# Both ends of a slot-ordered attention and FFN kernel written out as one list per engine

## The reference, cut to what matters

```
x = x + xattn(layernorm(x), ctx, mask)      # softmax over 120 keys, masked scores set to 1e-9
x = x + ffn(layernorm(x))
def bitlinear(x, w, b):                     # activations to 8 bit per row, weights to -1, 0, 1
    xq = act_quant(rmsnorm(x));  wq = weight_quant(w)
    return einsum('bsd,fd->bsf', xq, wq) + b
ffn(x) = bitlinear(gelu(bitlinear(x, w1, b1)), w2, b2)
```

## Time and profile before

| | |
|---|---|
| runs | 709.9, 712.62, 714.48 us; median 712.62 |
| the profiled execution | 713.07 us; span 711.3 us |
| mean granted TensorE clock | 0.988 |
| busy, share of the span | TensorE 92%, VectorE 83%, ScalarE 74%, GpSimd 72% |

### The profile page before, as it was taken

One profiled execution on the slowest core, in us unless ns is written; L12 is line 12 of the kernel. 1 busy time (PEld: TensorE's weight loads), 2 busy tenths in 40 slices (PEclk: granted clock), 3 DMA queues, 4 the chain that ended last, 5 costly groups with the idle time before them and its releaser, 6 DMA issues.

```text
span 711.3 us, 13969 instructions
## 1 busy us (share of the span) xinstructions
PE 653.6 (92%) x4894; PEld 428.6 (60%) x4894; DVE 591.6 (83%) x1056; ACT 529.4 (74%) x1462; POOL 511.0 (72%) x653
## 2 busy tenths in 40 slices
PE   7787889899999999999998999999999998888887
PEld 6555776556665666656655676566665674455544
DVE  6567587889798988999788988999798888888784
ACT  2474557868888678867997678867988778888554
POOL 2294867668777797768776797768777667887872
PEclk9988999999999999999999999999999999999999
DMA  8971120331324332342145332351122333334225
GB/s 295 376 261 70 32 95 24 53 105 37 81 68 127 81 82 68 79 116 47 49 68 127 81 82 66 68 138 39 55 60 67 82 67 68 67 68 68 57 58 146
DMA packets 109284, 65.38 MB, mean 92 GB/s; under 512 B 90855, under 2 KB 90855, under 8 KB 108575
## 3 DMA queue, kind: packets, MB, share of 16 engines
q1 hardware_dynamic: 108159, 64.49, 36.0%
q10 hardware_dynamic: 1056, 0.00, 0.1%
HBM read 35.12 MB, written 8.39 MB: 61 GB/s over the span
## 4 chain that ended last, share of the span: by engine, by line
PE 43%; DVE 29%; ACT 14%; issue 6%; DMA 3%; POOL 3%; SPq 1%; DVEq 0%; ACTq 0%; POOLq 0%
PE ps_a L458 14%; PE ps_z L560 7%; PE ps_y L581 5%; ACT prob L756 5%; DVE yw L959 5%; PE ps_a L531 4%; PE ps_a L488 3%; PE ps_t L519 3%; DVE hid L979 3%; DVE yq L962 2%; ACT hid L763 2%; DVE nmax L936 2%; DVE ps_s L933 2%; DVE hs L986 2%; DVE oT_l L898 2%
## 5 line engine op out<-in xcount | busy, mean ns | idle before, releaser
L1242 POOL TENSOR_TENSOR prob<-prob,pinv 128x480 f32<-128x480 f32 x128 | 126.3, 987 | 116.4 <-DVE pinv L941 112.7
L756 ACT ACTIVATE prob<-ps_s,nmax 128x120 f32<-128x120 f32 x512 | 180.4, 384 | 23.1 <-DVE nmax L936 22.8
L560 PE MATMUL ps_z<-w1T,q_xT 128*128 128x512 bf16 x476 | 123.4, 382 | 7.1 <-DMA q_xT<-q_x 7.0
L756 ACT ACTIVATION_READ_ACCUMULATOR prob<-ps_s,nmax 128x1 f32 x512 | 117.3, 229 | 0.0
L979 DVE SCALAR_TENSOR_TENSOR hid<-ps_z,y_deq,b_row 128x512 f32<-128x512 f32 x116 | 86.4, 745 | 27.9 <-PE ps_z L560 27.9
L581 PE MATMUL ps_y<-w2T,q_hT 128*128 128x512 bf16 x448 | 106.0, 379 | 0.0
L933 DVE COPY_PREDICATED_SCALAR ps_s<-hidden_key,masked_c 128x480 f32 x128 | 89.6, 700 | 6.2 <-PE ps_s L509 6.2
L519 PE MATMUL ps_t<-ident,prob 128*120 128x128 f32 x512 | 78.7, 277 | 12.3 <-ACT probT L728 10.6
L936 DVE TENSOR_REDUCE nmax<-ps_s 128x4 f32<-128x480 f32 x128 | 84.2, 658 | 4.4
L728 ACT COPY probT<-ps_t 120x512 f32<-120x512 f32 x128 | 79.5, 621 | 8.6 <-PE ps_t L519 8.4
L519 PEld LDWEIGHTS ps_t<-ident,prob 128*120 128x120 f32 x512 | 59.6, 138 | 32.9 <-ACT probT L728 20.6
(11 more groups left out here) (195 smaller groups left out, 1430.5 us busy)
## 6 DMA issues: line engine op xcount, KB each, us to landing
x<-in_x_dram SPq DMA_DIRECT2D x32, 256.0 KB, 2.7
out_dram<-x SPq DMA_DIRECT2D x32, 256.0 KB, 3.0
xn<-in_x_dram SPq DMA_DIRECT2D x7, 1024.0 KB, 5.2
hid<-in_L_ffn_w_dram SPq DMA_DIRECT2D x4, 1024.0 KB, 8.8
w2T<-in_L_ffn_w_dram SPq DMA_DIRECT2D x2, 1024.0 KB, 12.4
ctx_k<-in_ctx_dram SPq DMA_DIRECT2D x8, 240.0 KB, 3.7
ctx_k<-in_mask_Bx1xSxS_ik_dram SPq DMA_DIRECT2D x7, 240.0 KB, 2.8
xn<-in_x_dram SPq DMA_DIRECT2D x4, 256.0 KB, 4.6
```

The costliest lines, as they stand in the source:

```text
L560: last = nc.tensor.matmul(bank[:], q_xT[:, k % 3, i], w1T[:, i, c * CH:(c + 1) * CH], start=(i == 0), stop=(i == KD - 1))
L756: last = nc.scalar.activation(prob[:, n % 3, g * S2:(g + 1) * S2], ps_s[n % HG][:, g * S2:(g + 1) * S2], ACT.Exp, bias=nmax[:, n % 4, g:g ...
L1242: gp.tensor_tensor(pr, pr, pinv[:, n % 4].unsqueeze(2).to_broadcast([P, HG, S2]), ALU.mult).then_inc(s["prob_ready"], 1)
```

## The change

The five engines' loops now run only slots 26 to 105 as before. Slots 0 to 25 and slots 106 to 127 with the drain are written out as lists of the same steps, one list for each of SyncE, TensorE, ScalarE, VectorE and GpSimd, each in its own order. Every step of the slots is in the lists once. Beyond the order: `total_weights(0)` is called before the last `project_q(0, 3)`; piece 7 is summed on ScalarE instead of VectorE; `sum_abs(2)` moves ahead of `evac_q(0, 1)`; loads that stood in a slot (pieces, x, mask, context) become functions with the same waits; `stay_busy` is gone with its 38 transposes; `square_h(30)` moves ahead of `round_last` on ScalarE; the stores go out in the order 29, 28, 27, 30, 31; and some waits are added that keep the small ring buffers safe in the new orders (in `ln2_stats`, `h_scale`, `y_factor`, `h_factor`, `square_h`, and semaphores of their own for the last transposes). The diff, cut: of the lists the parts that are spoken of below stand here.

```diff
@@ -91,9 +92,9 @@
     ROUND_POOL_AT = {0: (1,), 2: (2,), 3: (3,), 7: (5,), 8: (6,), 9: (7,), 11: (4,)}
     ROUND_DVE = ()
     ROUND_POOL = (0, 1, 2, 3, 5, 6, 7, 4)
-    SUM_ACT = (0, 2, 4, 6)
-    SUM_ACT_AT = {2: 4, 4: 6}
-    SUM_DVE_AT = {4: 7, 6: 5}
+    SUM_ACT = (0, 2, 4, 6, 7)
+    SUM_ACT_AT = {3: 4, 4: 6, 6: 7}
+    SUM_DVE_AT = {6: 5}
     TOTAL_AT = 7
     SCALES_AT = 7
 
...
@@ -302,6 +304,11 @@
         def _(sp):
             def load_piece(p):
                 m, j = divmod(p, 4)
+
+                if p == 5:
+                    sp.wait_ge(s["wo_split"], 1)
+                elif p >= 6:
+                    sp.wait_ge(s["wT_full"], 4 * (p - 5))
                 if m == 0:
                     dst, src = piece_buf[p].rearrange("p (c d) -> p c d", d=D), w1_v[j]
                 else:
...
-            for n in range(NU):
+
+            load_piece(6)
+            load_piece(5)
+            load_residual(0)
+            load_residual(1)
+            load_piece(7)
+            load_x(2)
+            load_residual(2)
+            load_residual(3)
+            load_mask(1)
+            load_ctx(2)
+            load_residual(4)
+            turn_x(0)
+            load_residual(5)
+            turn_x(1)
+            load_x(3)
+            turn_x(2)
+            turn_h(0)
+            store(0)
+            turn_x(3)
+            turn_h(1)
+            load_mask(2)
+            for n in range(26, 106):
                 slot(n)
...
             turn_h(29)
             turn_h(30)
             turn_last(0)
+            store(29)
             turn_last(1)
-            for k in range(27, NT):
-                store(k)
+            store(28)
+            store(27)
+            store(30)
...
@@ -583,8 +642,8 @@
                     last.then_inc(s["y_full"], 1)
 
             def total_weights(m):
-                pe.wait_ge(s["abs_act"], 2 * (m + 1))
-                pe.wait_ge(s["abs_dve"], 2 * (m + 1))
+                pe.wait_ge(s["abs_act"], (2, 5)[m])
+                pe.wait_ge(s["abs_dve"], (2, 3)[m])
                 wait(pe, "xT_low", 2)
...
 
-            def stay_busy(times):
-
-                wait(pe, "x2_ready", NT)
-                for _ in range(times):
-                    nc.tensor.transpose(ps_a[:, 0:P], ident[:], ident[:])
...
@@ -679,34 +730,211 @@
             first_q(wq_l, xnT_h, 2).then_inc(s["a_full"], 1)
             turn_keys(0)
             for g in range(1, G):
+                if g == G - 1:
+                    total_weights(0)
                 project_q(0, g)
-            total_weights(0)
-            for n in range(NU):
+
+            scores(0)
+            turn_piece(0, (0, 1))
+            turn_piece(0, (2, 3))
+            project_ctx(0, "v", wv_s)
+            turn_ctx(1)
+            turn_piece(1, (0, 1))
+            turn_piece(1, (2, 3))
+            turn_piece(2, (0, 1))
+            turn_probs(0)
+            turn_piece(2, (2, 3))
+            project_ctx(1, "k", wk_s)
+            turn_xn(1, 0)
+            scores(1)
+            turn_probs(1)
+            turn_piece(3, (0, 1))
+            turn_piece(3, (2, 3))
+            turn_probs(2)
+            turn_xn(1, 1)
+            turn_probs(3)
+            project_ctx(1, "v", wv_s)
+            turn_xn(1, 2)
+            total_weights(1)
+            turn_probs(4)
+            attend(0)
+            turn_xn(1, 3)
+            scores(2)
+            turn_keys(1)
+            turn_probs(5)
+            project_q(1, 0)
+            turn_piece(4, (0, 1))
+            turn_probs(6)
+            project_out(0)
+            turn_piece(4, (2, 3))
+            turn_probs(7)
+            turn_piece(5, (0, 1))
+            project_q(1, 1)
+            turn_piece(5, (2, 3))
+            attend(1)
+            turn_probs(8)
+            turn_piece(6, (0, 1))
+            project_q(1, 2)
+            scores(3)
+            turn_piece(6, (2, 3))
+            turn_probs(9)
+            project_out(1)
+            turn_piece(7, (0, 1))
+            turn_probs(10)
+            turn_piece(7, (2, 3))
+            project_q(1, 3)
+            turn_probs(11)
+            turn_ctx(2)
+            ffn_up(0, 0)
+            turn_probs(12)
+            attend(2)
+            ffn_up(0, 1)
+            scores(4)
+            turn_probs(13)
...
+            attend(31)
             ffn_up(29, 0)
-            turn_probs(NU - 1)
+            ffn_up(29, 1)
+            ffn_up(29, 2)
+            project_out(31)
+            ffn_up(29, 3)
+            ffn_up(30, 0)
+            ffn_up(30, 1)
             ffn_down(27, 0)
-            attend(31)
-            ffn_up(29, 1)
-            project_out(31)
-            ffn_up(29, 2)
-            ffn_up(29, 3)
+            ffn_up(30, 2)
+            ffn_up(30, 3)
             ffn_down(27, 1)
-            for c in range(FC):
-                ffn_up(30, c)
             ffn_up(31, 0)
-            stay_busy(12)
-            for c in range(1, FC):
-                ffn_up(31, c)
-            for k, times in ((28, 0), (29, 16), (30, 10), (31, 0)):
-                stay_busy(times)
-                for half in range(2):
-                    ffn_down(k, half)
+            ffn_up(31, 1)
+            ffn_up(31, 2)
+            ffn_up(31, 3)
+            ffn_down(28, 0)
+            ffn_down(28, 1)
+            ffn_down(29, 0)
+            ffn_down(29, 1)
...
@@ -858,18 +1091,179 @@
             evac_keys(0)
             act.wait_ge(s["bias_ready"], 1)
             evac_q(0, 0)
+            sum_abs(2)
             evac_q(0, 1)
-            sum_abs(2)
             evac_q(0, 2)
+
             evac_q(0, 3)
-            for n in range(NU):
+            evac_piece(0, 0)
+            exps(0)
+            round_wo()
+            evac_piece(0, 2)
+            exps(1)
+            evac_turn(("c", 1, 0))
+            evac_piece(1, 0)
+            sum_abs(4)
+            evac_piece(1, 2)
+            evac_piece(2, 0)
+            exps(2)
+            sum_abs(6)
+            exps(3)
+            evac_probs(0)
+            evac_turn(("x", 1, 0))
+            evac_piece(2, 2)
+            evac_keys(1)
+            evac_probs(1)
+            evac_piece(3, 0)
+            sum_abs(7)
+            evac_probs(2)
+            exps(4)
+            evac_piece(3, 2)
+            evac_turn(("x", 1, 1))
+            evac_probs(3)
+            exps(5)
+            exps(6)
+            evac_turn(("x", 1, 2))
+            exps(7)
+            evac_turn(("x", 1, 3))
+            evac_o(0)
+            evac_probs(4)
...
             gelu_last(0)
             gelu_last(1)
             round_h(30)
+            square_h(30)
             round_last()
-            square_h(30)
             square_last(0)
...
@@ -947,6 +1341,8 @@
 
             def ln2_stats(k):
                 t = k % T
+                if k < T or k >= NT - 10:
+                    wait(dve, "ydeq_ready", k - 3)
                 wait(dve, "x2_ready", k + 1)
                 v.bn_stats(out=bn2[:, t], in_=x2[:, x2_at(k)]).then_inc(s["ln2_part"], 1)
                 wait(dve, "ln2_part", k + 1)
...
@@ -982,6 +1380,8 @@
 
             def h_scale(k):
                 t = k % T
+                if k < T or k >= NT - 10:
+                    wait(dve, "hdeq_ready", k - 3)
                 wait(dve, "gelu_done", k + 1)
                 v.tensor_reduce(out=hs[:, 3, t:t + 1], in_=hidden(k), op=ALU.max, axis=AX_X,
                                 apply_absolute_value=True).then_inc(s["h_abs"], 1)
...
-                    dve.wait_ge(s["bias_in"], 48)
+            ln1_stats(1, 0)
+            ln1_stats(1, 1)
+            softmax_max(0)
+            evac_piece(0, 1)
+            softmax_max(1)
+            invert_sums(0)
+            ln1_stats(1, 2)
+            evac_piece(0, 3)
+            split_wo()
+            invert_sums(1)
+            ln1_stats(1, 3)
+            evac_piece(1, 1)
+            softmax_max(2)
+            evac_piece(1, 3)
+            add_bv(0)
+            evac_piece(2, 1)
+            softmax_max(3)
+            evac_piece(2, 3)
+            invert_sums(2)
+            sum_abs(5)
+            xT_low(1, 0)
+            softmax_max(4)
+            evac_piece(3, 1)
+            invert_sums(3)
+            evac_piece(3, 3)
+            softmax_max(5)
+            softmax_max(6)
+            xT_low(1, 1)
+            invert_sums(4)
+            softmax_max(7)
+            add_bv(1)
+            weight_scales(1)
...
+            evac_up(29, 3)
             ln2_stats(31)
             ln2_scales(31)
-            evac_up(29, 2)
-            evac_up(29, 3)
-            for c in range(2):
-                evac_up(30, c)
+            evac_up(30, 0)
+            evac_up(30, 1)
+            evac_up(30, 2)
+            evac_up(30, 3)
             h_scale(29)
-            for c in range(2, FC):
-                evac_up(30, c)
+            h_scale(30)
             evac_up(31, 0)
             evac_up(31, 1)
-            h_scale(30)
             evac_up(31, 2)
             evac_up(31, 3)
             abs_half(0)
```

(38 more changed lines are left out.)

694 lines of the change are left out of this document (627 added, 67 removed).

## The result

The changed kernel takes 689.6 us as a median of four runs (687.14 to 691.9), the kernel before on the same chip 712.14 (four runs). The ratio is 0.968, with an interval of 0.964 to 0.973: 3.2% faster, where 687 us (a ratio of 0.964) was forecast. Ratios leave out executions more than 1.5% above the fastest of the same kernel (one of x_open, 712.9, and one of the kernel before beside it, 725.7); medians and ranges hold them. The profiled execution after took 687.14 us with a span of 685.3 and a mean granted clock of 1.00; before it was 713.07, 711.3 and 0.988.

The account below looks back on a forecast made before the run. TensorE fills the middle (97%); outside it the engines wait on each other's order, with VectorE's work the bound in the tail. 711.3 - 17.5 (opening) - 8.5 (tail) = 685.3 us span, with 1.8 above span 687; range 681 to 693.

Parts of the forecast that it names:

- The walk up to scores(4): Opening lists followed: 11.0 us gained at scores(2), 17 us ahead at scores(4).
- scores(4) to slot 26: Rest of the opening lists: 39 us instead of 40.7, ending at 138.5; lead 19 us, taken as 17.5.
- The edges at 157.6 and 579.8: Cuts of the profile before that the prediction used for the middle stage, where TensorE is busy 97%.
- The bounds, 8.5 to 22.7: Opening's gain: 22.7 us if TensorE never idles after 98.5; 8.5 if half of 11.0 and 3 of the rest come.
- The middle: Slots 26 to 105, order unchanged and TensorE full: 422 us, the lead carried through unchanged.
- The tail: Slot 106 to the last gelu input: 105 us instead of 113.6, VectorE 94% packed, 8.5 us gained.
- Behind the last gelu input: The end of the kernel: nothing won, again 17.9 us, with round_h(30) behind both gelu_last.
- The added waits and stay_busy: Added waits cost zero (2 to 3 us if wrongly ordered); removing stay_busy's 38 transposes at the end costs 0.
- The clock rival: At the end, TensorE's clock drops for want of stay_busy: 7 us more, 694 us; chance 0.08.
- The sum: Whole kernel: 711.3 - 17.5 - 8.5 = 685.3 us of span, 687 us forecast.
- the range: Whole kernel: forecast 681 to 693 us, chance 0.60.

Follow-up runs that it names:

- x_open: New lists for slots 0 to 25 only, with slots 26 to 127, the drain and stay_busy as in the kernel before; 706.7 us, ratio 0.987.
- x_total: The changed kernel with the first total of the weight sums back behind all of q(0), as before the change; 690.9 us, ratio to before 0.970.
- x_sums: The kernel before, in slot order throughout, with only the sum and total edits and the waits added to the steps; 711.1 us, ratio 0.996.
- x_swap: The changed kernel with exps(24) ahead of gelu(2) in ScalarE's opening list; 689.6 us, ratio to before 0.967.
- x_swap2: The changed kernel with exps(24) ahead of gelu(2) and load_x(3) between turn_x(2) and turn_h(0); 685.5 us, ratio to before 0.963.
- x_tail: The kernel before up to slot 105, with the new lists only for slots 106 to 127 and the drain; 702.4 us, ratio 0.986.
- x_warm: The kernel before with 26 idle transposes in slot 0 and 28 in slot 4, where TensorE waits; 712.2 us, ratio 0.997.
- x_seam2: The changed kernel with load_x(3) between turn_x(2) and turn_h(0) in place of ahead of both; 688.9 us, ratio to before 0.965.

## Why the prediction was right, and where it was not

**The walk up to scores(4): right.** Predicted were the first total at 27.4, rounding from 28.4, scores(1) 50.5, the second total 60.9, scores(2) 64.4, scores(4) 98.5 to 100. The trace has 27.39, 28.50, 50.25, 61.46, 64.57 and 100.36. TensorE was busy 35.48 of 35.8 us from scores(2) to scores(4), so the bound taken there, that it hardly waits, held. x_total bears out the first link (the total sets the pieces, the pieces set scores(2)), and x_sums shows that both halves, the sums and the order, were needed: 5.3 and 6.0 us.

**scores(4) to slot 26: the step that failed.** It put the end at 138.5 and the lead at 17.5; the lead was 12.9. Two mistakes. The lead was taken on TensorE alone, whose list puts some of its steps early (its lead by issued matmuls was 19.0 at the 944th), while the slot order starts from all engines: VectorE came to slot 26 with 12.9 in hand. And the walk stopped at scores(4), so it did not meet the two waits behind it, load_x(3) ahead of turn_x(2) (1.5 us of TensorE) and exps(24) behind gelu(2) (2.5 us of VectorE, 2.0 of TensorE). x_swap and x_swap2 show the second to be worth 1.4 us and the first 0.8 once the second is gone: 2.2 of the 4.6. The other 2.4 may come of reading the lead on one engine; no run shows it. The edges at 157.6 and 579.8, taken for slots 26 and 106, were off, the first by 7 us (turn_probs(23) at 164.6) and the second by more than 8 (slot 108 is at 571.3), which hid where the seam lies. The bounds, 8.5 to 22.7, held the value.

**The middle: 422 and the lead carried through.** From scores(8) to scores(14) and again from scores(18) to scores(26) the two traces keep their distance to 0.1 us (12.9 and 15.1 to 15.2). Between scores(14) and scores(18) before took 81.0 us and after 78.8, TensorE having waited 1.2 us for v_s and 1.0 for q_xT in before, 0.8 and nothing in after. That is 2.2 us that the prediction did not have. Of the other twelve profiles x_tail has 81.1, the rest 78.8 to 79.2, x_sums and x_warm among them, whose order is the old one but which come there 3.5 to 6.5 us earlier than before. So it is no gain of the lists; why the two latest kernels lose 2 us at that place stays open.

**The tail: mechanism right, term too small.** Predicted 8.5 us with VectorE packed to 94%. From scores(27) to the last gelu input it is 12.0 in these two profiles, with VectorE at 101.30 of 110.10 us, 92%, where before it had 104.55 of 122.10, 86%. Two things make up the difference: VectorE's work between these two marks is 3.2 us less after, some steps lying on the other side of a mark, and it is packed closer, though to 92 and not 94%. The waits that made, 5.0 us for the turned q_x and 4.9 for probT, are nearly gone; the list of TensorE's waits from 556.3 to 666.4 us after has no probT at all, and of the transfers only

```profile
PE ps_s L617 <- DVE wv_s L1377: 1.7, 1, 1.7
...
PE ps_s L617 <- DMA q_xT<-q_x: 0.6, 1, 0.6
```

with VectorE, the engine that was to become the bound, now first in it. x_tail gives 11.6 by itself.

**Behind the last gelu input: 18.9 instead of 17.9.** The chain that ended last, after (start, length, what; to be held against the earlier trace rows):

```profile
661.22 1.98 POOL hid L1891
...
663.23 1.92 ACT xn L1004
...
665.16 4.68 DMA q_hT<-xn
...
669.98 3.61 PE ps_s L640 x16
...
673.69 3.61 PE ps_s L640 x16
677.30 3.47 PE ps_y L640 x16
```

I had taken the chain of before, gelu_last, round_h(30), its transpose and two ffn_down. In the new order it is round_h(29) that is late, in two instructions on GpSimd and ScalarE, so ffn_down(29) starts at 669.98 and three ffn_down stand one behind the other, 10.7 us. "Again 17.9" held the wrong instruction late, at a cost of 1.0.

**The added waits and stay_busy: zero, and nothing speaks against it.** The added waits of the FFN factors stand only at tiles 0 to 3 and 22 to 31. x_sums and x_tail carry those of tiles 0 to 3 through the old order and x_warm does not have them; from scores(2) to scores(8), with one fall of the clock in each, the three take 119.3, 119.3 and 119.4 us, so there they cost nothing that shows. In the tail they were not tried by themselves. stay_busy back in (x_busy) changed nothing that can be measured. The clock rival (694) had no place: 1.00 to the end in the profile after.

**The sum** came out as 685.3 of span, to the tenth what was measured, by terms that were not: the opening 4.6 and the end 1.0 too good, against 2.2 in the middle and, by the marks at scores(27) and the last gelu input, 3.5 in the tail. The agreement is a cancellation; the range, not the point, is what the working had earned. The median of 689.6 stands 2.5 above the profiled execution; the three other runs had a mean clock of 0.996 or 0.997, the profiled one 1.00.

**What the working left out: the clock of the kernel before.** Its runs follow their mean granted clock: in the 13 runs beside x_sums 710.4 us at 0.993, 710.3 to 714.0 at 0.988, 717.2 at 0.981, 719 at 0.974, 725.7 at 0.967, about 0.6 us for each 0.001; the runs on the two other chips, 17 and 11, give 0.5. The changed kernel's sixteen stood at 0.993 to 1.00 and spread over 6 us instead of 15. A part of the 3.2% is thus clock: the kernel after has fewer of the holes behind which it fell. x_warm puts it at about 4 us in the opening; for the tail no run tells it apart.

## What to carry to other kernels

Follow a lead to the place where the old order takes over again, and read it there on the engine that arrives last, not on the busiest one: what one engine's list has drawn forward is not yet won. An order list that ends in front of a loop has a seam, and the steps on both sides of it are worth the same walk as the beginning (here two exchanged pairs of steps, worth 2.2 us in the profile and 3.3 in the medians, whose intervals still overlap). In an order written by hand every transfer belongs to the list too: late it holds the whole engine that reads it, early it holds the small transfer behind it.

## What the runs showed of the hardware that was not expected

One idle piece of TensorE of 2.94 us was followed by products at half speed in x_sums (1.89 us for what takes 1.02), while the same piece at the same instruction in x_warm was not. In the same way a wait of about 2 us for oT_l(5) had a fall of the clock behind it in x_seam2 and none in the kernel after. The same old tail, entered 8 to 13 us earlier, was granted the full clock in one run of x_open and less in others, and in the two profiles with several falls it took 6 to 7 us more. A DMA transpose of q_x, 1.2 us of issue, landed 5.6 us after it when a load of 1 MB had been issued 0.4 us ahead of it, and 2.4 us after it without. A change between gelu and exponentials costs ScalarE a table load of 1.28 us each time (three in x_swap where the kernel after has one), and with it TensorE waited 0.7 us more for probT. The Trainium skill, "ScalarE: Activation LUTs", section on what the load costs, has the same 1.28 us for the load and puts 1.38 of drain on top; in this trace exponentials and gelu lie 1.31 us apart around a load, so that no drain shows.
